# Deformable convolution block: the first strip's offsets prepared in the second stage, the tables in the first, and an entry to the third stage that waits for the flag alone

## The reference, cut to what matters

```python
fine = gn(x)                                      # x: 4 x 64 x 64 x 256, group norm, 32 groups
coarse_up = resize(coarse, (B, 64, 64, 256), 'bilinear')
attn = sigmoid(mean(fine, (1, 2)) @ attend_w)
fine_cal = (fine * (attn + 1)) @ select_w
align = concat([fine_cal, coarse_up * 2]) @ offset_w
om = conv3x3_same(align, om_w, om_b)              # 216 channels: 8 groups x 9 taps x (y, x, mask)
off, mask = om[..., :144], sigmoid(om[..., 144:])
# for each pixel, group and tap: coarse_up sampled bilinearly at (y + ky + off_y, x + kx + off_x),
# times mask; then 9 taps x 256 channels are contracted with dcn_w
out = x + relu(sampled @ dcn_w + dcn_b) + fine_cal
```

## Time and profile before

| what | value |
|---|---|
| median of 3 runs | 3083.11 us (3080.71 to 3084.54) |
| the profiled execution, its time | 3079.35 us |
| the profiled execution, its span | 3077.7 us |
| mean granted TensorE clock | 0.984 |
| busy: PE, weight loads | 2976.8, 2616.0 us |
| busy: DVE, ACT, POOL | 2490.5, 1490.2, 244.7 us |

### The profile page before, as it was taken

One profiled execution on the slowest core, in us unless ns is written; L12 is line 12 of the kernel. 1 busy time (PEld: TensorE's weight loads), 2 busy tenths in 40 slices (PEclk: granted clock), 3 DMA queues, 4 the chain that ended last, 5 costly groups with the idle time before them and its releaser, 6 DMA issues.

```text
span 3077.7 us, 85071 instructions
## 1 busy us (share of the span) xinstructions
PE 2976.8 (97%) x33798; PEld 2616.0 (85%) x33798; DVE 2490.5 (81%) x4298; ACT 1490.2 (48%) x2776; POOL 244.7 (8%) x445
## 2 busy tenths in 40 slices
PE   6999999999999938999999999999999999999998
PEld 6989999989999937888888888888888888888887
DVE  5678888878888878888888888888888888888881
ACT  0132222222222226666666666666666666666662
POOL 2000000000000000100101000011000101001010
PEclk9999999999999969999999999999999999999999
DMA  6343343323333242333332333422333323332332
GB/s 214 111 139 51 56 88 45 63 45 67 60 47 57 31 75 43 59 68 68 71 65 56 66 67 60 80 58 62 59 69 66 72 64 66 59 67 57 66 64 52
DMA packets 452687, 210.23 MB, mean 68 GB/s; under 512 B 230804, under 2 KB 447396, under 8 KB 452132
## 3 DMA queue, kind: packets, MB, share of 16 engines
q1 hardware_dynamic: 423092, 160.08, 28.6%
q10 hardware_dynamic: 24600, 27.96, 2.8%
q0 software_dynamic: 4608, 16.78, 1.4%
HBM read 104.80 MB, written 55.23 MB: 52 GB/s over the span
## 4 chain that ended last, share of the span: by engine, by line
PE 61%; DVE 1%; SPq 1%; DMA 1%; issue 0%; ACTq 0%; POOL 0%; ACT 0%; POOLq 0%; DVEq 0%
PE eb L1634 34%; PE tb L1190 16%; PE vb L1212 10%; PE eb L1225 1%; PE tb L1109 1%; SPq L1104 0%; DMA win<-cpad 0%; DMA rt<-r_d 0%; DVE wt L1184 0%; DVE part L905 0%; SPq L1302 0%; SPq L514 0%; DMA om_s<-om_d 0%; DMA om_d<-omT 0%; DVE part L926 0%
## 5 line engine op out<-in xcount | busy, mean ns | idle before, releaser
L1634 PE MATMUL eb<-val,wd 128*128 128x256 f32 (+1 forms) x4680 | 1217.2, 383 | 3.6 <-POOL gate L1404 3.6
L1195 ACT COPY wtT<-tb 128x512 f32<-128x512 f32 x1152 | 666.2, 585 | 616.6 <-PE tb L1190 615.1
L1634 PEld LDWEIGHTS eb<-val,wd 128*128 128x128 f32 x4680 | 793.0, 190 | 123.4 <-issue 56.7
L1184 DVE TENSOR_TENSOR wt<-taps_all 128x768 f32<-128x768 f32 x768 | 698.7, 951 | 24.0 <-PE tb L1190 21.7
L1190 PE MATMUL tb<-ident,wt 128*128 128x128 f32 x4608 | 695.5, 274 | 15.0 <-DVE wt L1184 12.2
L1190 PEld LDWEIGHTS tb<-ident,wt 128*128 128x128 f32 x4608 | 570.7, 141 | 124.0 <-DVE wt L1184 13.9
L640 PE MATMUL conv<-fine,wf 128*108 128x256 f32 x4464 | 571.1, 288 | 6.9 <-DVE fine L866 4.4
L640 PEld LDWEIGHTS conv<-fine,wf 128*108 128x108 f32 x4464 | 550.8, 173 | 22.8 <-issue 17.3
L1567 DVE COPY val<-vb 128x432 f32<-128x432 f32 (+1 forms) x384 | 212.5, 553 | 254.6 <-PE vb L1212 254.3
L1212 PE MATMUL vb<-wtT,win 64*32 64x144 f32 x16384 | 315.6, 287 | 2.3 <-DVE val L1567 1.1
L1212 PEld LDWEIGHTS vb<-wtT,win 64*32 64x32 f32 x16384 | 239.5, 106 | 46.7 <-issue 45.0
(11 more groups left out here) (154 smaller groups left out, 2319.1 us busy)
## 6 DMA issues: line engine op xcount, KB each, us to landing
val<-val SPq DMA_DIRECT2D x128, 396.0 KB, 3.8
win<-cpad SPq DMA_DIRECT2D x304, 64.0 KB
om_s<-om_d SPq DMA_DIRECT2D x1143, 12.0 KB
chunk<-in_x SPq DMA_DIRECT2D x32, 512.0 KB, 5.3
xchunk<-in_x SPq DMA_DIRECT2D x32, 512.0 KB, 4.2
r_d<-r POOLq DMA_DIRECT2D x32, 512.0 KB, 3.2
rt<-r_d SPq DMA_DIRECT2D x63, 256.0 KB, 5.0
out<-ot ACTq DMA_DIRECT2D x63, 256.0 KB, 2.1
```

The source lines that it names most:

```text
L1184: return nc.vector.tensor_tensor(wt[b][:, PER * d:PER * (d + 1), WQ * u:WQ * (u + 1)].rearrange("p k (a b) -> p k a b", a=WIN), of_rows(0) ...
L1195: return nc.scalar.copy(dst, src) if e == "act" else nc.vector.tensor_copy(dst, src)
L1634: done = nc.tensor.matmul(eb[q][:, 256 * fo:256 * fo + rows], wd[:, half, k, 128 * fo:128 * fo + 128], val[:, half, k, at:at + rows // W, ...
```

## The change

- The coordinates are loaded by ACT in the first stage, behind the bias loads, and the tables are made there by VectorE (`set_tables`, at m = 5). The general path gets tables of its own, `plain_y` and `plain_x`.
- The tiles that locate a strip (`om_s`, `om`, `pos`, `lo`, `mask`, `coef`) lie in `xchunk0` and `xchunk1`, the second stage's tiles for x, and are used by both stages. The helpers `load_offsets`, `turn_offsets`, `keep_offsets`, `sigmoid`, `positions` move to `strip_steps`, unchanged but for arguments.
- In the second stage SP loads strip 0's offsets when the last x is turned, ahead of the last four batches' stores, and strip 1's ahead of the very last batch's. In batch g = 29 TensorE turns strip 0, ACT keeps it and takes the sigmoid, VectorE locates it.
- The stores of `om_d` leave `ended`. SP waits for them ahead of the window of image 1, which now lies in `shared`, the memory of `omT`.
- At the entry ACT loads the bias alone (`CONSTS` 16, was 96). SP asks for rows 0 to 3 of the first window and POOL for rows 4 to 7. The weights `wd` are asked for after strip 1 is kept, and TensorE waits for them ahead of its first `project`.

```diff
 # first stage, ACT
+            by_row = coords_d.rearrange("(j r c) n -> r j c n", j=BLK, r=4)
+            for r in range(4):
+                act.dma_start(coords[32 * r:32 * r + 32], by_row[r]).then_inc(coords_loaded, 16)
             act.wait_ge(early.loaded, EARLY)
...
 # first stage, DVE
+        def set_tables(dve):
...
+            dve.wait_ge(coords_loaded, 16 * 4)
+            for table, name in ((tables.plain_y, "y"), (tables.base_y, "y"), (tables.plain_x, "x"), (tables.base_x, "x"),
+                                (tables.ctr_x, "ctr_x"), (tables.ctr_all, "ctr_all")):
+                nc.vector.tensor_copy(table[:], plain[name][:, 0:table.shape[1]]).then_inc(based, 1)
...
+                        nc.vector.tensor_copy(turned_rows[:, :, r, to:to + m], rows[:, :, r, own:own + m]).then_inc(based, 1)
...
+                if m == 5:
+                    set_tables(dve)
 # second stage, SP
             loop(sp, batch)
+            w(sp, "x_turned", 2 * NS)
+            strip.load_offsets(sp, 0, True, strip.sems["om_loaded"])
             for n in range(BEHIND):
+                if n == BEHIND - 1:
+                    sp.wait_ge(strip.sems["batched"], 1)
+                    strip.load_offsets(sp, 1, True, strip.sems["om_loaded"])
                 store_offsets(B - 1, SB - BEHIND + n)
-            for i in range(2):
-                sp.wait_ge(om_stored[i], 16 * B * STORES)
 # PE (prepares(g): g == NS - 3, the last image's batch 29)
                     coarse_groups(unit, i, n % 2, range(3))
+                    if prepares(g):
+                        pe.wait_ge(strip.sems["om_loaded"], 16 * OM_LOADS)
+                        strip.turn_offsets(tb).then_inc(strip.sems["batched"], 1)
                     turn_x(g + 3, n + 3)
                     convolve(g, n, 1)
 # ACT
                     keep_groups(unit, i, n % 2, range(3), g - n % 2 + 1, 2 * b + 1 if n == 0 else 0)
+                    if prepares(g):
+                        act.wait_ge(strip.sems["batched"], 1)
+                        strip.keep_offsets(tb).then_inc(strip.sems["tb_out"], 1)
+                        act.wait_ge(strip.sems["tb_out"], 1)
+                        strip.sigmoid().then_inc(strip.sems["masked"], 1)
 # DVE
                     add_products(b, n, 1)
+                    if prepares(g):
+                        dve.wait_ge(strip.sems["masked"], 1)
+                        strip.positions(dve, nc.vector, tables.base_y, tables.base_x, 0, strip.sems["pchain"], 0)
+                        dve.wait_ge(strip.sems["pchain"], NPOS)
+                        nc.vector.tensor_tensor(strip.coef[0], strip.lo[:, 0], strip.mask, ALU.mult
+                                                ).then_inc(strip.sems["coef_ready"], 1)
...
-        return [(s["flagged"], 4), (r_stored, 16 * NS), (s["padded"], 16 * 2)] + [(st, 16 * B * STORES) for st in om_stored]
+        return [(s["flagged"], 4), (r_stored, 16 * NS), (s["padded"], 16 * 2)], [(st, 16 * B * STORES) for st in om_stored]
 # third stage, SP
+                    if b == 1:
+                        all_offsets_stored(sp)
...
-                load_offsets(sp, 0, True, sems["om_loaded"], (0,))
-                for s in range(1, 3):
-                    w(sp, "batched", s)
-                    load_offsets(sp, s, True, sems["om_loaded"])
+                windows(sp, 0, 0, range(4), sems["win_whole"])
+                w(sp, "batched", 2)
+                load_offsets(sp, 2, True, sems["om_loaded"])
...
-                whole_windows(0)
 # POOL
+                windows(pool, 0, 0, range(4, WIN), sems["win_first"])
                 g.memset(val[:, :, 0:3, 0:2, 1:W + 1], 0.0).then_inc(sems["cleared"], 1)
 # ACT
-                load_offsets(act, 0, True, sems["om_loaded"], (1,))
-                load_weights(act)
-                act.wait_ge(consts, CONSTS)
-                keep(0, 0, 0)
                 for hx in range(2):
                     lengths(0, 0, hx)
                     slopes(0, 0, hx)
                 keep(1, 1, 1)
+                load_weights(act)
+                act.wait_ge(consts, CONSTS)
 # DVE: the tables' steps and locate(0, 0) go
-                dve.wait_ge(tabled, TABLES)
...
-                dve.wait_ge(based, BASED)
-                locate(0, 0)
                 dve.wait_ge(sems["pchain"], NPOS)
 # PE
+                            if isinstance(s, int) and s == 0:
+                                w(pe, "win_first", 16 * 8)
+                            w(pe, "win_whole", 16 * (16 * (s // SI) + 8))
...
-                for s in range(2):
-                    offsets_turn(s, s, s)
-                weights_loaded(pe)
+                offsets_turn(1, 1, 1)
...
             entered(pe)
-            pe.wait_ge(consts, CONSTS)
             choose(pe, fast_pe, gen_pe)
```

More of the change, by code:

```diff
@@ L390, in statistics_and_weights, with offsets_and_calibration @@
         return [(merged_out, len(products)), (x_turned, 2 * NS)], (counted, 2 * NS), early, gate_steps
-def offsets_and_calibration(nc, block, sem, ended, counted, early, gate, x, coarse, cpad, wf, wc, scale, shift, om_d, r_d, flag):
+def offsets_and_calibration(nc, block, sem, ended, counted, early, gate, x, coarse, cpad, wf, wc, scale, shift, om_d, r_d, flag, shared, chunks, strip, tables):
     NRING, TERMS = 16, 5
@@ L418, in offsets_and_calibration @@
         part = sb("part", [OMC, 2, 2, 4, VW])
-        omT = [sb(f"omT{i}", [OMC, 2, 8, W]) for i in range(2)]
+        omT = [shared[0:OMC, 1024 * i:1024 * (i + 1)].rearrange("p (o y x) -> p o y x", o=2, y=8) for i in range(2)]
         ext = sb("ext", [OMC, 2, NS])
@@ L676, in _ @@
             pe.wait_ge(s["flagged"], 1)
+            pe.wait_ge(strip.sems["tb_out"], 1)
             for o in range(2):
@@ L1012, in sample_and_project @@
         sb = lambda name, shape, dt=f32: ctx.enter_context(nc.sbuf_tensor(name, shape, dt))
[L1013 to L1016, removed]
+        base_y, base_x, ctr_y, ctr_x, ctr_all, plain_y, plain_x = tables
+        (om_s, om, pos, lo, mask, coef, consts, strip_sems, wait, hold, load_offsets, turn_offsets, keep_offsets, sigmoid,
+         positions) = strip
         wd = sb("wd", [128, CH, NK, C])
@@ L1031, in sample_and_project @@
         NSUM = NK * 256
-        win_both = [sb(f"win{i}", [128, 2 * BLK * 128]) for i in range(2)]
+        win_both = [sb("win0", [128, 2 * BLK * 128]), shared]
         wins = [t[:].rearrange("p (j c) -> p j c", c=128) for t in win_both]
@@ L1106, in turn_offsets @@
-        def turn_offsets(b):
-            for hx in range(2):
-                for part, (c, m) in enumerate(((0, 5 * TAPC), (5 * TAPC, 4 * TAPC))):
-                    last = nc.tensor.transpose(tb[b][:, NOM * hx + c:NOM * hx + c + m], om_s[0:m, part, hx],
-                                               ident[0:m, 0:m])
-            return last
-        def keep_offsets(b):
-            return nc.scalar.copy(om[:].rearrange("p x c -> p (x c)"), tb[b][:, 0:2 * NOM])
-        def by_half(table):
-            return table.rearrange("p x (u k c) -> p x u k c", u=2, k=NK)
@@ L1282, in bank_no, with windows @@
                 return batch_no(s if isinstance(s, int) else p, hx, i) % 2
+            def windows(e, b, at, rows, signal):
+                for a in rows:
+                    for u in range(2):
+                        part = WQ * u + WIN * (a % WIN)
+                        src = bass.AP(tensor=cpad.tensor, offset=at + a * PADC * C + 128 * u,
+                                      ap=[[C, WIN], [2 * C, 2 * BLK], [1, 128]])
+                        e.dma_start(wins[b % 2][part:part + WIN], src).then_inc(signal, 16)
             def sp_fast(sp):
@@ L1679, in slot @@
                         if known(target, 0, ST + 1):
+                            if isinstance(target, int) and target == 0 and first == 0 and i == 0:
+                                weights_loaded(pe)
                             if first == 0 and i == 0:
```

248 lines of the change are left out of this document (128 added, 120 removed).

## The result

The changed kernel takes 3067.95 us (median of 5 runs, 3067.01 to 3072.08) against 3084.54 us (5 runs, 3080.71 to 3088.89): ratio 0.9950, 95% interval 0.9935 to 0.9966. Measured once more, with other runs of before, it was 3070.73 (6 runs, 3066.83 to 3075.00) against 3084.39: 0.9951 (0.9934 to 0.9968). So it is 14 to 17 us faster, where 12.7 was forecast; both medians lie inside the range.

A forecast was written before the change was run, and what follows sets the result against it. The kernel's end was taken to hang on when VectorE can start third-stage work; -21.9 + 1.7 + 2.3 + 1.7 + 0.5 + 2.8 + 0.8 - 0.6 = -12.7 us, so 3079.35 becomes 3066.7 (3070.4 against the median), range 3063 to 3077.

The forecast's parts named there:

- entry: Start of third stage: flag to first distances falls from 22.99 to 1.1 us, a gain of 21.9 us (21.5 to 22.3).
- coordinates: First stage: four loads, 0.595 MB, share the full DMA with `omw`, costing 1.7 us (zero to 3.5).
- tables, pause of TensorE: First stage, m = 5: `set_tables` delays a split, so TensorE stands for 2.3 us (1.9 to 3.1).
- clock behind that pause: First stage: TensorE's clock falls after the tables' 2.3 us pause, charged 1.7 us (0 to 2.2).
- positions: End of second stage: VectorE locates strip 0 behind `add_products` of g = 29, 2.8 us on the chain.
- clock and slack ahead of the last batch: End of second stage: TensorE's idle before 1075.54 lowers its clock; `convolve` grows 1.3, 0.47 is slack: 0.8 us (0 to 1.2).
- Rival 3: Third-stage entry: something equally late as the last stores still holds VectorE; 7.94 us of gain go, 3078 us; chance 0.05.
- Rival 1: First stage: coordinates fit beside `omw` and the clock stays full, giving -16.1 us, 3067; chance 0.20.
- Cover: End of second stage: SP's 18 loads per strip and ACT's delayed `keep_fine` stay hidden; nobody waits.
- Rival 2: Third stage: SP late with strip 2's offsets or windows, a new wait; some 6 us give 3076; chance 0.07.
- Rival 4: Third-stage entry: GpSimd's software queue starves on its half of the first window, making the kernel slower; chance 0.05.
- The sign of being wrong: VectorE idle over 2 us anew between first distances and first `project`, or the flag more than 12 us later.

The follow-up runs named there:

- the experiment: Changed kernel with the four coordinate loads issued behind the rims' split instead of at 15 us: 3062.22 us (4 runs), 5.7 to 8.5 us faster.

## Why the prediction was right, step by step

| step | forecast | in the trace |
|---|---|---|
| entry | -21.9 | -21.9 (22.99 to 1.06) |
| coordinates | +1.7 | +2.7; 3.5 by the experiment |
| tables, pause of TensorE | +2.3 | +2.1 (1.88 idle) |
| clock behind that pause | +1.7 | 0; 1.7 in one trace of eight |
| turning | +0.5 | +0.3 |
| positions | +2.8 | +2.8 |
| clock and slack ahead of the last batch | +0.8 | +1.3 |
| window | -0.6 | -0.6 |
| clearings against the scaling | not foreseen | +2.6 |
| second stage up to the turning, 1.5 of it the clock | not foreseen | -2.0 |
| sum to the first `project` | -12.7 | -12.4, with 0.3 for a slower first round of merges |

That the sums agree to 0.3 us is in part luck. The entry, the tables, the positions and the window came out as forecast, but the coordinates (+1.0), the last batch (+0.5) and the clearings (+2.6) cost more, and the clock behind the tables (-1.7) and in the second stage (-2.0) gave about as much back. The best case of the range adds up to -18.5, not -18.4, which changes nothing.

*What holds the kernel.* The change was to be worth what it moves VectorE's first distances. It did: -14.4 there and -12.4 at the first `project`. That the stretch behind it keeps its length is less sure. The prediction called a third stage of another length a cause not seen, and it was 5.0 us longer in this trace; the twelve traces with the change take 1900.6 to 1906.2 us for it and the one of before 1900.5, and about 1.1 us stands at a fixed place in all twelve.

*The entry* is right to a tenth. Rival 3 (another thing holds the entry) is out: putting the stores back costs 7.2 us.

*The coordinates* were right in kind and too small. Bytes over the measured rate gave 1.7 us; the trace shows 2.7 and the removal 3.5. The bound of 3.5, from a slower stretch, came closer, but nothing ties it to this place. The Trainium skill's rule of a round between the queues (DMA: Bandwidth & Descriptors, Queues, rings and completion order) agrees in kind: `omw` landed 23.0 us after its issue with the four loads beside it, and 20.5 and 19.3 without them, which queues served one after the other in the order of issue wouldn't show. Why the loads cost up to twice what their bytes would, no run shows.

*The tables.* The pause is where it was put, 1.88 us long, with 0.27 for the broken row. It vanished when the tables moved by two rounds, which costs nothing, for VectorE idles 3.4 us there.

*The clock* was the weak step. I charged it by the pause's length: the forecast pause of 2.3 us was nearer to 2.42 than to 1.71. The pause itself was 1.88, so by the same measure nothing should have been charged, and in seven of eight traces nothing was lost. But the length doesn't settle it: the same program with the same pause has full clock in one execution and a fall in the next. A pause of 1.88 us cost 1.68 once in eight, those of 2.4 us 1.3 to 3.0 in 22 of 26 cases. At that rate a charge of 0.2 us (1.68 / 8) would have been right; nothing on record before told the rate. By luck, the second stage up to the turning gave 2.0 back. 1.5 of it are the first `convolve`, 10.47 us before and 9.00 after: the granted clock was 0.66 from 170 to 175 us, ahead of a wait for VectorE that shrank from 3.96 to 2.34 us by it, instead of from 175 to 180, in the `convolve`. The other 0.5 lie in small pieces that I didn't follow.

*Rival 1* (a cheap first stage) had the clock right, in this trace, and the coordinates wrong. The times can't tell its -16.1 from the sum's -12.7, for the two medians are 13.7 and 16.6 us below before; the traces tell them apart, by `omw` at 29.84 to 30.31 us.

*Cover.* SP's 18 loads ran from 1019.85 to 1028.8 and disturbed no store; ACT's delayed `keep_fine` was hidden (VectorE still waited 1.92 us for TensorE). The 18 loads took 9.0 us where 7.4 were reckoned; the next stores began at 1030.98. Rival 2 has no support: TensorE waited for no DMA between 1108 and 1170.

*Rival 4* took the right pair of engines and the direction that costs nothing. I asked whether VectorE can hold up GpSimd's loads. It can, where they meet: in the four traces with the memsets first, one of the eight took 1.00 to 1.04 us to issue instead of 0.59, and nobody waited. What cost time was the other direction. It was GpSimd's clearings, which the loads had pushed into VectorE's way, that held up VectorE. The step that missed it is "VectorE's and ACT's order of work stays": their order did, but GpSimd's clearings moved behind 4.7 us of loads, and I did not ask what they would now run beside. The sign of being wrong, an idle time of VectorE over 2 us, doesn't catch it either: the 2.13 us lie inside an instruction and count as busy. The Trainium skill has the rule (SBUF — State Buffer, Who interferes with whom): GpSimd and VectorE in a two-port mode exclude each other, and the one that comes second is blocked while the other's instruction runs. The trace agrees for the clearings (2.89 against 0.76 us), and shows more: the scaling waited not for one of them but for all that were left, and ended 0.6 us behind the last.

*Open.* Why the medians say 14 to 17 us and the landmarks 12.4 stays open; the spread of the third stage, 5.7 us, is larger than that gap. So does the cause of the pause 836 to 839 us behind the first `project`, and why `omw` comes 0.8 us earlier with late coordinates than before.

## What to carry to other kernels

Work that leaves a stretch where everybody waits must land in a pause of the engine that runs it: the same tables cost 2.1 us at m = 5 and nothing at m = 3, the same positions 3.6 to 4.4 us behind `add_products` and about 0.8 ahead of it, the same coordinates 3.5 us beside a full DMA and nothing 30 us later. Before a queue of GpSimd is given DMAs, look at what its own instructions, pushed back by them, will run beside on VectorE. And where two profiled executions differ by less than the clock's luck, compare landmarks, not spans; a pause that stands at the same landmark in every trace of a program is not luck.

## What the runs showed of the hardware

- A scaling of VectorE (tensor_scalar, 128x1152, float32) beside GpSimd's memsets took 2.87 to 2.91 us instead of 0.76, in every one of the six traces where they met; tensor_tensor (0.75) beside the same memsets, where these came first, kept its time.
- The other way round, the GpSimd DMA issue that ran beside that scaling took 1.00 to 1.04 us instead of 0.59 in the four traces where they met, and ended 0.14 us behind it in the trace shown; the scaling kept its 0.76.
- What TensorE's clock costs behind pauses of 1.9 to 2.5 us differs between executions of the same code, from nothing to 3.0 us a time; the end of the first stage moved from 131.99 to 135.78 us, mostly with it, over the seven traces with the same first stage, and a change of a few us can't be read from one trace's span.
- TensorE's pauses without a releaser in the third stage came to 0.3 us before and to 0.8 to 3.3 us in the twelve traces with the change; one of them, of 0.85 to 1.40 us, stands at the same matmul in all twelve.
